# Six landing slots instead of five, fifteen kept pairs instead of sixteen, and the second hop's rows kept in SBUF, in a four-layer graph kernel

## The reference

```
h = LN(x);  Ax = adj @ h
x = x + 1 - 0.1*h - 0.01*sum(h*Ax, axis=1)                              # layer 0
h = LN(x);  for k in (0, 1): h = tanh(concat(adj @ h, h) @ W[k])
x = x + h                                                               # layer 1, two hops
h = LN(x);  s = h @ weight;  w = mask * 0.5**(places from the right), the last 100 nonzeros of a row
x = x + w @ s + bias                                                    # layer 2
h = LN(x);  u = tanh([h, t] @ W1 + b1) @ W2 + b2;  hB = h @ B.T
x = x + u + adj @ hB - rowsum(adj) * hB                                 # layer 3
```

## Time and profile before

| | |
|---|---|
| runs, median (lowest to highest) | 710.43 us (709.11 to 710.64) |
| the profiled execution, its own time | 709.48 us |
| its span | 707.4 us |
| TensorE busy (matmul) | 665.8 us, 94% |
| VectorE busy | 467.7 us, 66% |
| ScalarE busy | 191.5 us, 27% |
| GpSimd busy | 115.2 us, 16% |
| granted TensorE clock | 1.00 of full speed throughout |
| DMA | 260.72 MB, mean 369 GB/s |
| loads into `land` / into `cache` | 220 / 16, 1 MB each |
| pieces of x rows stored and loaded (128 KB) | 32 stored, 24 loaded |

### The profile page before, as it was taken

How to read it: one execution, slowest core, us unless ns; L and a number is a source line. 1 busy time by engine, 2 the same in 40 slices (tenths; PEclk the granted TensorE clock), 3 DMA queues, 4 the chain that set the end, 5 groups by cost and what they waited for, 6 DMA issues and landing times.

```text
span 707.4 us, 10670 instructions
## 1 busy us (share of the span) xinstructions
PE 665.8 (94%) x3907; PEld 265.2 (37%) x3920; DVE 467.7 (66%) x798; ACT 191.5 (27%) x295; POOL 115.2 (16%) x132
## 2 busy tenths in 40 slices
PE   2999999989999999999999997999988899999997
PEld 0423333323333333333443332444444433333332
DVE  7777667777799999876888878999888820000000
ACT  2101111111211111110101005799888821111111
POOL 4111011111100000001322332132221211211111
PEclk9999999999999999999999999999999999999999
DMA  8999999997599999959999995999999559999992
GB/s 359 422 411 413 413 413 415 416 417 315 192 341 400 422 422 420 377 201 396 411 420 418 418 399 198 350 397 415 413 398 384 202 216 354 415 408 420 416 409 117
DMA packets 47524, 260.72 MB, mean 369 GB/s; under 512 B 6577, under 2 KB 16561, under 8 KB 17265
## 3 DMA queue, kind: packets, MB, share of 16 engines
q1 hardware_dynamic: 40824, 254.03, 89.1%
q10 hardware_dynamic: 6648, 6.02, 2.6%
HBM read 254.38 MB, written 5.64 MB: 368 GB/s over the span
## 4 chain that ended last, share of the span: by engine, by line
PE 54%; DMA 23%; DVE 15%; issue 3%; POOL 3%; ACT 1%; SPq 0%; DVEq 0%; ACTq 0%
PE accA L1303 40%; DMA land<-adj_blocks 21%; DVE uS L1068 6%; DVE uS L1099 4%; PE work L1338 3%; PE accA L1351 2%; DMA cache<-adj_blocks 2%; PE work L1205 2%; POOL rstd L734 2%; PE work L1321 1%; PE work L1179 1%; PE work L1266 1%; PE accA L1272 1%; POOL tS L744 1%; DVE wS L552 1%
## 5 line engine op out<-in xcount | busy, mean ns | idle before, releaser
L1303 PE MATMUL accA<-land,X 128*64 128x512 f32 x1536 | 369.4, 599 | 18.3 <-DMA land<-adj_blocks 15.3
L1303 PEld LDWEIGHTS accA<-land,X 128*64 128x64 f32 x1536 | 103.2, 137 | 188.8 <-issue 153.4
L1099 DVE TENSOR_SCALAR uS<-land 128x1024 bf16<-128x1024 f32 (+1 forms) x192 | 133.6, 735 | 33.1 <-DMA land<-adj_blocks 31.7
L1068 DVE TENSOR_TENSOR uS<-uS,land 128x512 f32<-128x512 f32 x190 | 135.8, 715 | 10.7 <-DMA land<-adj_blocks 0.7
L1303 PE MATMUL accA<-cache,X 128*64 128x512 f32 x512 | 125.0, 593 | 3.5 <-ACT accS L819 2.5
L554 ACT ACTIVATE wS<-work 128x1024 uint16<-128x1024 f32 x112 | 107.3, 1034 | 13.5 <-PE work L1338 12.6
L1054 DVE TENSOR_TENSOR zS<-uS,work 128x256 f32<-128x256 f32 x8 | 3.4, 421 | 122.7 <-PE work L1205 106.4
L741 POOL TENSOR_TENSOR hS<-tS 128x256 f32<-128x256 f32 x24 | 23.2, 966 | 349.9 <-DVE tS L935 349.9
L1338 PE MATMUL work<-uS,triA 128*128 128x512 bf16 x246 | 73.9, 379 | 4.7 <-DVE wS L552 2.9
L1351 PE MATMUL accA<-wS,X 128*128 128x512 bf16 x253 | 75.1, 379 | 0.6
L1303 PEld LDWEIGHTS accA<-cache,X 128*64 128x64 f32 x512 | 37.1, 137 | 67.4 <-issue 55.1
(11 more groups left out here) (89 smaller groups left out, 385.0 us busy)
## 6 DMA issues: line engine op xcount, KB each, us to landing
land<-adj_blocks SPq DMA_DIRECT2D x220, 1024.0 KB, 9.0
cache<-adj_blocks SPq DMA_DIRECT2D x16, 1024.0 KB, 15.0
x_rows<-zS ACTq DMA_DIRECT2D x16, 128.0 KB, 7.2
xin<-x_rows ACTq DMA_DIRECT2D x16, 128.0 KB, 7.1
x_rows<-zS SPq DMA_DIRECT2D x8, 128.0 KB, 10.3
xin<-x_rows SPq DMA_DIRECT2D x8, 128.0 KB, 10.0
out_rows<-zS ACTq DMA_DIRECT2D x8, 128.0 KB, 6.6
uS<-counts ACTq DMA_DIRECT2D x60, 4.0 KB
```

The costliest lines, as they stand in the source:

```text
L1068: nc.vector.tensor_tensor(total, total, of[:, i * W:(i + 1) * W], ALU.add)\
L1099: nc.vector.tensor_scalar(masks(b)[0:rows, :], block_of(p, c, b)[0:rows, :], 0.0, None, ALU.not_equal)\
L1303: last = nc.tensor.matmul(accA[k * D:(k + 1) * D, c % 2, :], tile(X[p % 2], TQ * q + k), of[:, k * W:(k + 1) * W], start=(b == 0), stop=(b ...
```

## The change

`land` gets a sixth slot, and in its place pair 4 of chunk 4 is no longer kept, so that it is loaded in every sweep. The first step of L1A takes its pairs in another order. The sums of x after the second hop (L1B) are no longer stored and loaded: VectorE writes them over the finished part of `Z` (the space of the weights wS), ScalarE copies them into X[0] at the end of L1B (keep_rows), and GpSimd and VectorE use them there in L2. VectorE leaves the two evacuations of L2's first step to ScalarE. The residual, the variance and the norm of L2 come one block sooner. The stores and loads that SyncE issued between loads move accordingly.

```
 def cached_pairs(c):
-    return (0, 4)
+    return (0,) if c == 4 else (0, 4)
-FIRST = {L0: (1, 0, 2, 3, 5, 4, 6, 7), L1A: (2, 3, 5, 0, 4, 6, 1, 7), L2: (1, 2, 3, 5, 0, 4, 6, 7)}
+FIRST = {L0: (1, 0, 2, 3, 5, 4, 6, 7), L1A: (1, 2, 3, 5, 0, 4, 6, 7), L2: (1, 2, 3, 5, 0, 4, 6, 7)}
-LAND = 5
+LAND = 6
 def evac_on_dve(c):
-    return (10, 14) if c == 0 else (3, 13)
+    return (3, 13) if c else ()
-STAGES_L2 = {0: 2, "join0": 4, "join1": 5, 4: 6, 5: 8, 6: 10, 7: 13, 8: 15}
+STAGES_L2 = {0: 2, "join0": 4, "join1": 5, 4: 5, 5: 7, 6: 9, 7: 13, 8: 15}
+ROWS_KEPT = {6: 5, 8: 4, 9: 6, 10: 3, 12: 2, 14: 1}
...
-    rows_from = {L1B: x1_d, L2: x2_d, L3: x3_d}
-    rows_to = {L0: x1_d, L1B: x2_d, L2: x3_d, L3: out}
+    rows_from = {L1B: x1_d, L3: x3_d}
+    rows_to = {L0: x1_d, L2: x3_d, L3: out}
...
             else:
                 eng.wait_ge(nat_evac, nat_no(L1B, 2 * n + 1) + 1)
+                eng.wait_ge(rows_kept, NC - 1)
...
                 if p == L3 and c == 0:
                     rows_store(sp, L2, NC - 2)
-                    rows_load(sp, L2, NC - 1)
...
-                    if (p, c, j) == (L2, 1, 0):
-                        rows_store(sp, L1B, NC - 1)
-                    if (p, c, j) == (L2, 1, 4):
-                        rows_load(sp, L2, 0)
                     if p == L2 and c >= 2 and j == 3:
                         rows_store(sp, L2, c - 2)
-                        rows_load(sp, L2, c - 1)
...
                     if before[0] == L2:
-                        pool.wait_ge(rows_in, (rows_in_no(*before) + 1) * 16)
-                        nc.gpsimd.tensor_tensor(rows4(xin), rows4(xin), over_tiles("bias"), ALU.add).then_inc(biased, 1)
+                        rows = rows4(chunk(X[0], ch(*before)))
+                        if before[1] == 0:
+                            pool.wait_ge(rows_kept, NC - 1)
+                        nc.gpsimd.tensor_tensor(rows, rows, over_tiles("bias"), ALU.add).then_inc(biased, 1)
...
+            def keep_rows(k):
+                act.wait_ge(copy_used, copied_no(L1B, k) + 1)
+                act.wait_ge(swept, sweep_no(L1B, NC - 1, NQ - 1 - 2 * k) + 1)
+                nc.scalar.activation(chunk(X[0], k), chunk(Z, k), ACT.Copy).then_inc(rows_kept, 1)
             def main(p, c, b):
+                if (p, c) == (L1B, NC - 1) and b in ROWS_KEPT:
+                    keep_rows(ROWS_KEPT[b])
+                if (p, c, b) == (L2, 0, 0):
+                    keep_rows(0)
...
                         if p == L1B:
+                            z = chunk(Z if c < NC - 1 else X[0], c)
+                            rows_in_sbuf()
                             dve.wait_ge(tanh_done, tanh_no(p, c) + 1)
-                            nc.vector.tensor_tensor(zS[:, :], xin[:, :], natS[:, :], ALU.add).then_inc(copy_used, 1)
+                            if c == NC - 1:
+                                dve.wait_ge(swept, sweep_no(L1B, c) + 1)
+                            nc.vector.tensor_tensor(z, xin[:, :], natS[:, :], ALU.add).then_inc(copy_used, 1)
...
-                            nc.vector.tensor_tensor(rows4(tS), rows4(xin), parts[:, 0], ALU.add).then_inc(copy_used, 1)
+                            nc.vector.tensor_tensor(rows4(tS), rows4(chunk(X[0], ch(p, c))), parts[:, 0], ALU.add)\
+                                .then_inc(copy_used, 1)
```

More of the change, by code:

```diff
@@ L200, in rows_in_no, with rows_out_no @@
 def rows_in_no(p, c):
-    return row_no(p, c) - NC
+    return {L1B: c, L3: 8 + c}[p]
+def rows_out_no(p, c):
+    return {L0: c, L2: 8 + c, L3: 16 + c}[p]
 def norm_no(p, c):
@@ L276, in rows_by_sync @@
 def rows_by_sync(p, c):
-    return p == L2 and c < NC - 1 or (p, c) == (L1B, NC - 1)
+    return p == L2 and c < NC - 1
+ROWS_KEPT = {6: 5, 8: 4, 9: 6, 10: 3, 12: 2, 14: 1}
 LEFT_L1A = {"counts": 3, "weights": 4, "left": 6, "left out": 8}
@@ L332, in gnn_kernel @@
     x1_d = nc.dram_tensor("x1_rows", (P, NT * D), F32, kind="Internal").ap()
-    x2_d = nc.dram_tensor("x2_rows", (P, NT * D), F32, kind="Internal").ap()
     x3_d = nc.dram_tensor("x3_rows", (P, NT * D), F32, kind="Internal").ap()
@@ L567, in rows_load @@
         def rows_load(eng, p, c):
-            made = {L1B: L0, L2: L1B, L3: L2}[p]
-            if c or p != L1B:
-                last = (p, c - 1) if c else (made, NC - 1)
-                if last[0] == L3:
-                    eng.wait_ge(side_ready, last[1] + 1)
-                else:
-                    eng.wait_ge(copy_used, copied_no(*last) + 1)
-            eng.wait_ge(rows_out, 16 * (row_no(made, ch(made, ch(p, c))) + 1))
+            made = {L1B: L0, L3: L2}[p]
+            if p == L3 and c:
+                eng.wait_ge(side_ready, c)
+            elif p == L3 or c:
+                eng.wait_ge(copy_used, copied_no(L1B, NC - 1 if p == L3 else c - 1) + 1)
+            eng.wait_ge(rows_out, 16 * (rows_out_no(made, ch(made, ch(p, c))) + 1))
             eng.dma_start(xin[:, :], chunk(rows_from[p], ch(p, c))).then_inc(rows_in, 16)
@@ L582, in rows_store @@
                 eng.wait_ge(rows_ready, c + 1)
-            elif p == L1B:
-                eng.wait_ge(copy_used, copied_no(p, c) + 1)
             else:
@@ L697, in step @@
                             after_masks(PAIRS * pc + i)
+                if (p, c) == (L1A, 0):
+                    left_adjacency(NC - 1)
+                if (p, c) == (L3, 0):
+                    sp.wait_ge(w_used, NQ * NC)
+                    sp.dma_start(late_wts, wts_in[:, LATE_FROM:NCOLS]).then_inc(late_wts_in, 16)
+                    rows_back(1)
+                    rows_back(2)
             def rows_of(p, c, k):
@@ L1336, in triangle @@
                     weights_ready(tri_before(n))
+                elif n >= NQ:
+                    pe.wait_ge(rowsum_ready, 1)
                 for k in range(TQ):
```

21 lines of the change are left out of this document (7 added, 14 removed).

## The result

| | before | after |
|---|---|---|
| median of the runs, us | 710.64 (709.11 to 711.35, 5 runs) | 705.98 (705.08 to 706.86, 5 runs) |
| profiled execution, us | 709.48 | 706.86 |
| its span, us | 707.4 | 705.1 |

The ratio is 0.9933, with a 95% interval of 0.9917 to 0.995: faster by 4.7 us. The forecast was 701.6 us in a range of 697.5 to 706.5. The time lies in the range and the direction is right, but little more than half of the 8.1 us came. The profiled execution of before was 1.2 us under its median and that of after 0.9 us above, so the two profiles are 2.6 us apart where the medians are 4.7.

A forecast was written before the change was run, and what follows sets the result against it. Transfers were taken to bound L0, later L1B and L2 (close to VectorE), TensorE L1A and L3. Terms 2.0 + 2.2 + 2.4 + 1.5 = 8.1 us gave 701.6 us, range 697.5 to 706.5.

The forecast's parts named there:

- rival 3: Waits in L1A's start and at L2's end turn into others as long; only the bytes count: 4.6 us, 704.9 us; 18%.
- L1A's order: L1A's first step: two totals in each of VectorE's idle times remove two TensorE waits; 2.0 us, at worst 1.2.
- The slot and the pair: Sixth slot and seven loads on chunk 4: 5.5 us to spare carries the 2.1 us too much; counted at nothing.
- rival 1: Steps on chunk 4 stall once in each of four sweeps, 7.9 us in all; slower, 712.8 us; 6%.
- L1B without its stores: L1B: six stores fewer in the DMA-bound stretch bring it to TensorE's own pace; 2.2 us, between 1.2 and 3.0.
- L2 without its loads of rows: L2 from 461 to 560 us: six loads fewer at 0.40 us, transfers remaining the bound; 2.4 us.
- rival 4: L2 loses all its excess over VectorE's pace, 5.3 us; 11.0 us in all, 698.5 us; 15%.
- The norm one block sooner: L2's last step: GpSimd's root runs beside the masks, so TensorE's wait for the norm goes; 1.5 us, between 0 and 2.3.
- Rival 2: L2: VectorE's residual waits for TensorE's join, at worst a whole mask in 7 steps; 5.2 us back, 706.6 us; 12%.
- ScalarE's copies and evacuations: Eight copies, seven in L1B's last step, and two evacuations in L2's first step: counted at nothing, -0.5 to +1.5 us.
- L3, L0: L3 TensorE-bound with 0.4 us fewer on DMA: nothing; L0, at transfer speed, loses no byte and stays as it is.

The follow-up runs named there:

- slots alone: Kernel before with six slots, fifteen kept pairs and L1A's new first order; rows still through device memory, residual where it was: 708.79 us, ratio 0.9971.
- five slots: Kernel after with `LAND = 5`, sixteen kept pairs and the old first order of L1A: 707.08 us, ratio 0.9944 to the kernel before.
- the nine kernels: Those of the kernels run that share the same L1B, with seven loads on chunk 4 and no bias add in it: L1B took 124.8 to 126.3 us.
- chunk 0: Kernel after with pair 4 of chunk 0 left out of the kept ones instead of chunk 4's: 706.65 us, ratio 0.9942 to the kernel before.
- the last experiment: Kernel after with bias in ScalarE's copy, residual a block later, left rows in one DMA, plus counts rows sent to 64 partitions of an unused buffer: 702.67 us.

## Why the prediction was right, and where it was not

The direction and the range held, but the time is not in the range for the reasons that I gave: two terms of the sum were wrong, and what they missed in both directions partly cancelled. The 4.7 us that came are, to 0.1, what rival 3 gave (only the bytes count), and that is luck as well, since 1.6 us of them are L1A's waits, which it had at nothing. The last step of the sum has a slip: 701.4 us was worked out from the profiled execution, which lies 0.95 us under the median, so the forecast of the median should have been 702.3 us and not 701.6. Step by step:

*L1A's order*, 2.0 us: 1.6 measured (33.30 for 34.89 us in two steps, and 33.31 with slots alone). The first wait went, the second stayed at 0.73 of 0.87 us. That is nearer the bound of 1.2 which I had given for this case than the value I took.

*The slot and the pair*, nothing: wrong. The arithmetic of 5.5 us to spare against 2.1 took the median landing of 8.0 us, but in L1B landings already set the pace, and there is nothing to spare. L1B took 1.1 us more than with five slots in the profiled execution (126.33 and 125.20), and with slots alone there was such a wait in L1A too. How much of it is the seventh load is not shown: the nine kernels with this L1B took 125.7 us on the mean, 0.5 more than with five slots, and scatter over 1.5 us. This is rival 1, which I priced only for four sweeps at once, at 7.9 us; in the kernel after it came in one sweep and at a seventh of that at most.

*L1B without its stores*, 2.2 us: in its range where the seven loads are out of the way, 126.90 - 125.20 = 1.7 us with five slots, 1.8 with chunk 0. In the profiled execution of the kernel after 0.6 us were left of it, and by the mean of the nine kernels 1.2.

*L2 without its loads of rows*, 2.4 us with transfers still the bound: wrong twice, in opposite directions. The removal took L2 off the transfers (no wait for landings at 16.88 us a step; at 16.10, once the rest is mended, they bind only its last steps, with 16.4 to 17.2 us), which is most of rival 4. The late landings at a DMA share of 1.0 come in good part from the counts rows, as the last experiment shows; a sixth slot alone did nothing for L2. And the pace of the engines, which I took from before as 16.11 us, rose to 16.88. The failed sentence is "GpSimd's bias add no longer waits for a landing; that wait cost nobody anything". True, but a wait that goes moves the work behind it, and I did not ask what it would then run beside. It costs 0.43 us in each of seven steps, 3 us.

*The norm one block sooner*, 1.5 us: the wait at the end fell from 1.49 to 0.23 us, and the last step from 18.75 to 17.49, but with the residual back in its place that step is 17.98, so this part brought 0.5 us of it. And the residual at the join costs 0.35 us in each of the other steps. Undone, the kernel is as fast or faster (705.00). Rival 2 had the place right, and its price was between nothing and the worst case that I gave, 0.74 us a step.

*ScalarE's copies and evacuations*, nothing, with 1.5 us at the other end: the evacuations gain 1.5 us in L2's first step, and the left rows take back 1.1 in the second. ScalarE's copies are seven and not eight, six of them in L1B's last step; they take 0.42 us each and cost nothing that these runs show.

*L3, L0*, nothing: so it is.

In the profile this makes 1.6 + 0.6 + 1.1 = 3.3 us for L1A, L1B and L2 where I had 2.0 + 2.2 + 3.9 = 8.1. By medians, slots alone brought 2.1 us, the rows kept in SBUF with the evacuations 3.8 us more (705.00), and the sooner residual took 1 back, a difference within the intervals. What stays open: how much of L1B's waits is the seventh load and how much chance, and why one copy of the left rows lands after 2.6 us in one kernel and after 5.0 us in another.

## What to carry to other kernels

When a change removes a wait, write down when the waiting instruction will now run and what it will run beside; on GpSimd and VectorE above all, read the mean length of untouched instructions before and after. Equal steps at unequal transfer rates speak for an engine's loop, whatever the DMA share says. And once a bound is lifted, the sum is not made against the old pace: the next bound may have been moved by the same change.

## What the runs showed of the hardware

- An add of GpSimd (0.64 us) lengthens a VectorE instruction of 0.29 us that starts 0.08 us behind it to 0.71 us. The cost appears wherever the add stood just ahead of the norm: 0.43 us a step in L2, some 0.4 us a step in L1B, with the same 0.71 us.
- A scale-and-copy of 128x512 out of PSUM on ScalarE took 613 ns, and 704 ns with a column of biases; the steps did not grow by it, where the same add on GpSimd cost the kernel 3 us.
- At DMA shares of 1.01 to 1.03 two kernels that differ in the counts' target (and in masks of 127 or 128 partitions) waited for landings (13.4 to 15.7 us) or not (10.4 to 12.5 us), according to whether 4 KB pieces went to one partition or to 64: a full DMA share does not tell whether landings bind.
- Four small copies took SyncE 2.40 us to issue, one copy of the same rows 0.67 us; the one copy landed between 2.6 and 5.0 us after its issue, in five kernels.
- A 4 KB row into one partition left 2 completion events, a 1 MB pair over 128 partitions 16, and the same row over 64 partitions 16.
